# in_proj and x_proj behind the pair sums of a slot, in a fused Mamba and FFN kernel

## The chip, the cores and the metric

The kernel runs on one core of a Trainium2 chip. The metric is device time in microseconds from launch to end, the median of several runs. Matrix work runs on TensorE (PE; its weight loads are PEld), elementwise work and scans on VectorE (DVE), activations on ScalarE (ACT), the rest on GpSimd (POOL); SyncE (SP) issues the DMAs. All data is f32.

## What is computed

Four batches of 1024 tokens and 1024 channels. First a Mamba block: x is projected from the context (in_proj), goes through a short causal convolution and silu to u; x_proj makes from u the rows dt, B and C; then a scan along the tokens with 16 states for each channel, summed over the states with C. Its gate comes from the layer norm of x. Behind it stands an FFN with routing: logits over a whole batch choose two of eight experts, whose small hidden layers run on 16 heads, and a last 1024 x 1024 product with w3.

```python
x = einsum('ed,bld->bel', in_proj_w, ctx)            # in_proj
u = silu(causal_conv(x, conv_w) + conv_b)
x_dbl = einsum('ke,bel->bkl', x_proj_w, u)           # x_proj: dt_lo, Bm, Cm
delta = softplus(dt_proj_w @ dt_lo + dt_proj_b)
state = state * exp(delta * A) + (delta * u) * Bm    # for each token, 16 states
y = (state * Cm).sum(states) + D * u
x1 = x + y * silu(layernorm(x))
ffn: top 2 of softmax(layernorm(x1) @ switch_w); gelu MLP per head; (xn + o) @ w3 + b3
```

## The kernel before

The scan runs in 64 **steps**, 16 per batch: a step takes 512 tokens (half a batch, eight steps) and 128 channels. I number them 0 to 15 within a batch; steps 0 to 7 are the first half of the tokens, 8 to 15 the second. A step has eight **slots** q = 0 to 7, each for a pair of the 16 states. In a slot ScalarE makes two factors exp(delta A) (L1246); VectorE scans the two states (L1525) into one of three buffers `h`, and makes delta u times B for the next pair (L1501), except that in batch 0 TensorE makes it for five of the eight pairs (L948, from a transposed copy `duT`); GpSimd multiplies the pair with C (L865, "the product"); TensorE adds the pair to `yT` in PSUM (`sum_pair`, L962, "the sum"). A buffer `h` is free again three pairs later, when the sum is done.

Work for later steps is laid into slots by a table (`Schedule`): in_proj for the channels ten steps ahead (four matmuls of 512 columns, two passes each, L900) stands in slot 6 of most steps; in step 6 and step 14 slots 6 and 7 hold the two halves of x_proj for the next eight steps (L912), and in_proj follows in slot 0 of the next step. In_proj, x_proj, `v` (the matmul for delta, L921) and the transposes `zT` share PSUM bank S. In slot 1 (slot 2 of steps 7 and 15) of the next step ScalarE does the first tap of the convolution on in_proj's result (L1163 or L1172) and VectorE the other three (L1357). ScalarE's copies of the x_proj rows (L1184, L1185) stand at the head of slot 0, ahead of the exponentials. The FFN of one batch runs during the scans of the next: `hidden` (L1055), gelu on ScalarE (L1331, with a table load), `expert_out` (L1065), `out_add` (L1477), the logits (L1112) and the tiles with w3 (L1135).

Each engine is in order and goes through `slot(b, t)` for every batch b and slot t. For TensorE a slot had this order: in batch 0 the products with B; then a loop over the table's entries that holds in_proj, x_proj, zT, v, hidden and expert_out; in batch 0 in slot 7 the transposes of du_s (L929), which ScalarE copies to `duT` (L1209) in slot 0 of the next step, ahead of uD and of the next exponentials; then the sum of the pair one slot back (`sum_pair(g, q - 1)`, which waits for that pair's product); then a loop over the logits and tiles.

Of the kernel before, what the change touches and what calls it, by code (L numbers as in the profile page):

```python
# [16 lines left out]
J = DI // P  # L17
# [16 lines left out]
STEPS = TH * J  # L34
ALL = NB * STEPS
AHEAD = 10
# [223 lines left out]
PLAN = Schedule()  # L260


def build(nc, x, ctxT, w_inT, conv_w, conv_b, x_projT, dt_projT, dt_b, A_log, D, sw, sw_b,
# [4 lines left out]
    with ExitStack() as ctx:  # L268
# [210 lines left out]
        def count(b, *name):  # L479

            return PLAN.use[(b, *name)][1]
# [409 lines left out]
        def _(pe):  # L891
            e = pe

            def in_proj(loads, par, bank, wait):


                e.wait_ge(win_loaded[par], 1 + 16 * loads)
                e.wait_ge(evac[bank], 1 + wait)
                for k in range(DK):
                    mm = e.matmul(dense[:, bank, :], win[:, par, k, :], ctxs[:, k, :],  # L900
                                  start=(k == 0), stop=(k == DK - 1))
                mm.then_inc(xin_done, 1)
# [108 lines left out]
            def slot(b, t):  # L1011
# [9 lines left out]
                for what, *a in PLAN.slots[b][t]:  # L1021
# [35 lines left out]
                    elif what == "expert_out":  # L1057
# [7 lines left out]
                            mm = e.matmul(dense[HD * i:HD * i + HD, bank, :], w2s[:], hs_of(b, hp)[:, i, :],  # L1065
                                          start=True, stop=True)
                        mm.then_inc(o_done, 1)
                    elif what == "in_proj":
                        G = STEPS * b + a[0] + AHEAD
                        if G % J == 0:  # L1070
                            e.wait_ge(ctx_loaded, 1 + 16 * (G // J + 1))
                        in_proj((G - J) // 2 + 1, G % 2, S, count(b, *name))
                    elif what == "x_proj":
                        x_proj(c + 1, 1 - th, count(b, *name))
                    elif what == "x_proj_end":
                        x_proj_part(c + 1, range(J // 2, J))
                    elif what == "zT":
                        e.wait_ge(zn_done, 1 + g + 1)
                        e.wait_ge(evac[S], 1 + count(b, *name))
                        for k in range(TB):  # L1080
                            mm = e.transpose(dense[:, S, k * P:(k + 1) * P], xz[:, k * P:(k + 1) * P], ident[:])
                        mm.then_inc(zT_done, 1)
                    elif what == "v":
                        bo, th2, j2 = chunk_block(g + 1)
                        before_softplus(TH * bo + th2, j2, count(b, *name))
# [7 lines left out]
                    first_sum(g)  # L1093
                if b < NB and q >= 2:
                    sum_pair(g, q - 1)
                if b == 0 and q == SLOTS - 1:
                    times_b_at(N * g + 2 * q + 4)
                for what, *a in PLAN.slots[b][t]:
# [547 lines left out]
```

## Time and profile before

| | |
|---|---|
| three runs | 2474.52, 2473.86, 2465.63 us, median 2473.86 |
| the profiled execution | 2471.16 us, its span 2469.3 us |
| busy in the span | VectorE 2133.6 us (86%), TensorE 2013.5 (82%), ScalarE 1602.4 (65%), GpSimd 1445.2 (59%) |
| mean granted TensorE clock | 0.90 of full speed (2.4 GHz) |

The scans of the four batches fill the time from 95 to about 2283 us; after them a tail of 187 us finishes the FFN of the last batch, mostly on TensorE. A view of the profile that shows waits tells for how long an engine stood idle ahead of an instruction, and behind "<-" what released it. In the order of time a row may hold several instructions of one kind. A matmul's end in the trace is modelled and a little late, so work in sequence on TensorE is best timed from start to start.

### The profile page before, as it was taken

What the parts mean: (1) busy time and instruction counts of PE and PEld (TensorE: products, weight loads), DVE (VectorE), ACT (ScalarE), POOL (GpSimd) and SP (SyncE); (2) the same over time, 40 slices, a digit from 0 to 9 for tenths busy, and PEclk for the clock granted to TensorE, in tenths of its full rate; (3) what the DMA queues carried; (4) which work ended last, traced back from release to release, by engine and by line L of the source; (5) the groups of instructions that cost most, each with busy time, mean ns of one, the idle gap of its engine ahead of it and who ended that gap; (6) DMA issues with size and microseconds to landing.
All of it is one profiled execution on the core that took longest, in us unless ns stands there. A gap on an engine that the chain in (4) does not pass through costs nothing.

```text
span 2469.3 us, 32717 instructions
## 1 busy us (share of the span) xinstructions
PE 2013.5 (82%) x10776; PEld 1203.1 (49%) x10776; DVE 2133.6 (86%) x2712; ACT 1602.4 (65%) x2357; POOL 1445.2 (59%) x993
## 2 busy tenths in 40 slices
PE   6798888985757997996675897898685798797899
PEld 2677676653433553454453454454453455344344
DVE  5899789979999899998999899998999899999322
ACT  2677787656669868655667878855576857954500
POOL 0588677767756566566675566665775666665000
PEclk9899889997878998997888999899787899999899
DMA  5311434555612754566542464466460174578412
GB/s 174 128 37 52 150 99 148 188 162 169 246 37 103 261 166 133 161 204 203 188 155 74 140 232 152 147 224 199 154 239 26 60 253 145 164 251 283 168 56 72
DMA packets 200329, 383.01 MB, mean 155 GB/s; under 512 B 31553, under 2 KB 97089, under 8 KB 200162
## 3 DMA queue, kind: packets, MB, share of 16 engines
q1 hardware_dynamic: 196992, 380.47, 46.1%
q8 instruction: 86, 1.41, 0.2%
q10 hardware_dynamic: 3170, 0.47, 0.1%
q14 instruction: 81, 0.66, 0.1%
HBM read 346.80 MB, written 34.08 MB: 154 GB/s over the span
## 4 chain that ended last, share of the span: by engine, by line
PE 44%; DVE 19%; issue 17%; ACT 14%; POOL 3%; DMA 1%; DVEq 0%; SPq 0%; ACTq 0%; POOLq 0%
PE dense L1135 13%; PE dense L962 9%; DVE h L1525 9%; PE dense L900 5%; ACT dA L1246 4%; PE dense L948 3%; DVE dense L1501 3%; POOL h L865 3%; DVE u L1357 2%; PE dense L912 2%; PE dense L1112 2%; ACT L1213 2%; PE dense L921 2%; PE dense L1065 2%; PE dense L969 2%
## 5 line engine op out<-in xcount | busy, mean ns | idle before, releaser
L865 POOL TENSOR_TENSOR h<-h,Cb 128x1024 f32<-128x1024 f32 x512 | 1208.4, 2361 | 431.8 <-DVE h L1525 408.2
L1246 ACT ACTIVATE dA<-delta,Av 128x512 f32<-128x512 f32 x1024 | 703.1, 717 | 384.6 <-DVE h L1525 381.3
L962 PE MATMUL dense<-ident,h 128*128 128x128 f32 x4096 | 605.4, 299 | 165.0 <-POOL h L865 163.5
L962 PEld LDWEIGHTS dense<-ident,h 128*128 128x128 f32 x4096 | 521.1, 155 | 315.6 <-POOL h L865 225.8
L1525 DVE TENSOR_TENSOR_SCAN h<-dA,state,dense 128x512 f32<-128x512 f32 x512 | 627.4, 1263 | 31.0 <-issue 14.4
L1525 DVE TENSOR_TENSOR_SCAN h<-dA,dense 128x512 f32<-128x512 f32 x512 | 596.7, 1203 | 22.0 <-PE dense L962 8.5
L1501 DVE TENSOR_TENSOR dense<-dense,Bb 128x512 f32<-128x512 f32 x864 | 550.5, 682 | 1.6
L1135 PE MATMUL dense<-w3h,xT 128*128 128x512 f32 x832 | 386.0, 598 | 0.0
L859 POOL COPY state<-h 128x2 f32<-128x2 f32 x256 | 47.6, 186 | 336.6 <-DVE h L1525 335.1
L948 PE MATMUL dense<-Bb,duT 128*128 128x128 f32 x1280 | 179.9, 289 | 41.1 <-DVE h L1525 31.7
L1135 PEld LDWEIGHTS dense<-w3h,xT 128*128 128x128 f32 x832 | 147.9, 192 | 130.1 <-issue 130.1
L900 PE MATMUL dense<-ctxs,win 128*128 128x512 f32 x432 | 208.5, 628 | 2.2 <-ACT szT L1278 1.5
L948 PEld LDWEIGHTS dense<-Bb,duT 128*128 128x128 f32 x1280 | 160.4, 199 | 72.9 <-issue 65.6
L921 PE MATMUL dense<-dtaug,dtw 33*128 33x512 f32 x128 | 95.2, 832 | 110.2 <-DVE u L1357 108.5
L1357 DVE SCALAR_TENSOR_TENSOR u<-dense,cw,u 128x511 f32<-128x511 f32 (+2 forms) x192 | 140.7, 733 | 50.6 <-ACT u L1172 24.8
L1213 ACT ACT_TABLE_LOAD x113 | 145.0, 1283 | 2.0
L900 PEld LDWEIGHTS dense<-ctxs,win 128*128 128x128 f32 x432 | 84.2, 204 | 101.8 <-issue 101.8
L1112 PE MATMUL dense<-sww,row 128*32 128x256 f32 x1336 | 110.5, 417 | 1.2 <-ACT row L1287 1.2
L1065 PE MATMUL dense<-hs,w2s 128*64 128x512 f32 x224 | 72.8, 729 | 44.0 <-ACT hs L1331 41.4
L1202 ACT COPY dense<-du_s 128x512 f32<-128x512 f32 x64 | 37.5, 587 | 103.5 <-DVE dense L1501 103.3
L921 PEld LDWEIGHTS dense<-dtaug,dtw 33*128 33x128 f32 x128 | 24.5, 239 | 140.5 <-issue 140.4
L1487 DVE TENSOR_TENSOR res<-res,h 128x512 f32<-128x512 f32 x16 | 11.1, 691 | 88.1 <-PE dense L1135 88.1
(168 smaller groups left out, 2084.1 us busy)
## 6 DMA issues: line engine op xcount, KB each, us to landing
sww<-in_sw SPq DMA_DIRECT2D x167, 512.0 KB, 4.2
Cb<-bc_scratch SPq DMA_DIRECT2D x64, 512.0 KB, 6.1
Bb<-bc_scratch SPq DMA_DIRECT2D x54, 512.0 KB, 4.6
w3h<-in_sw SPq DMA_DIRECT2D x52, 512.0 KB, 8.2
w3h<-in_w3T SPq DMA_DIRECT2D x52, 512.0 KB, 5.2
row<-x_scratch SPq DMA_DIRECT2D x40, 512.0 KB, 4.5
xz<-in_x SPq DMA_DIRECT2D x64, 256.0 KB, 4.7
xt<-in_x SPq DMA_DIRECT2D x64, 256.0 KB, 3.9
```

Source lines behind the costliest of these rows:

```text
L865: e.tensor_tensor(h[:, s:s + 2, :], h[:, s:s + 2, :], Cb[:, 2 * q:2 * q + 2, :], ALU.mult).then_inc(prod_done, 1)
L900: mm = e.matmul(dense[:, bank, :], win[:, par, k, :], ctxs[:, k, :], start=(k == 0), stop=(k == DK - 1))
L921: e.matmul(dense[:, S, :], dtw[0:DR + 1, j * P:(j + 1) * P], dtaug[:], start=True, stop=True) \
L948: mm = e.matmul(dense[:, product_bank(g, n), k * P:(k + 1) * P], duT[:, g % 2, k, :], Bb[:, n, k * P:(k + 1) * P], start=True, stop=True)
L962: mm = e.matmul(yT[:, k, :], h[:, 2 * ((PAIRS * g + q) % RH) + i, k * P:(k + 1) * P], ident[:], is_transpose=True, start=False, stop=(q == ...
L1112: mm = e.matmul(dense[32 * n:32 * n + 32, F2, 0:32 * E], rows[:, lo:lo + 32], weights[:, :, 32 * n:32 * n + 32], start=first, stop=(k % TB ...
L1135: mm = e.matmul(dense[:, bank, :], xT_of(b, uu)[:, d, k * P:(k + 1) * P], w3[:, d, :], start=(b == NB and d == 0), stop=(d == J - 1), skip ...
L1213: e.preload_act_table_set("natural_log_exp_and_others")
L1246: e.activation(dA[:, i % RA, :], delta[:, st % 2, :], ACT.Exp, scale=Av[:, j * N + n:j * N + n + 1]).then_inc(dA_done, 1)
L1357: i = e.scalar_tensor_tensor(out=u[:, G % UR, s:T], in0=dense[:, bank, 0:T - s], scalar=cw[:, j, k:k + 1], in1=u[:, G % UR, s:T], op0=ALU. ...
L1501: e.tensor_tensor(dense[:, product_bank(g, n), :], du[:], Bb[:, n, :], ALU.mult).then_inc(duB_done, 1)
L1525: e.tensor_tensor_scan(h[:, 2 * ((PAIRS * g + q) % RH) + n % 2, :], dA[:, (N * g + n) % RA, :], dense[:, product_bank(g, n), :], state[:, ...
```

## The change

The three kinds of entries `in_proj`, `x_proj` and `x_proj_end` are taken out of TensorE's first loop and put into a loop of their own behind `sum_pair`, in the same slot. Waits, counts, banks and the table stay as they are, and so do the other engines' instructions. What stood behind these entries in the slot's first loop (`hidden`, `expert_out`, `turn`) and, in batch 0, the transposes of du_s in slot 7 now stand ahead of those of the same slot.

```diff
@@ -1065,15 +1065,6 @@
-                    elif what == "in_proj":
-                        G = STEPS * b + a[0] + AHEAD
-                        if G % J == 0:
-                            e.wait_ge(ctx_loaded, 1 + 16 * (G // J + 1))
-                        in_proj((G - J) // 2 + 1, G % 2, S, count(b, *name))
-                    elif what == "x_proj":
-                        x_proj(c + 1, 1 - th, count(b, *name))
-                    elif what == "x_proj_end":
-                        x_proj_part(c + 1, range(J // 2, J))
                     elif what == "zT":
@@ -1093,6 +1084,16 @@
                     first_sum(g)
                 if b < NB and q >= 2:
                     sum_pair(g, q - 1)
+                for what, *a in PLAN.slots[b][t]:
+                    if what == "in_proj":
+                        G = STEPS * b + a[0] + AHEAD
+                        if G % J == 0:
+                            e.wait_ge(ctx_loaded, 1 + 16 * (G // J + 1))
+                        in_proj((G - J) // 2 + 1, G % 2, S, count(b, what, *a))
+                    elif what == "x_proj":
+                        x_proj(c + 1, 1 - th, count(b, what, *a))
+                    elif what == "x_proj_end":
+                        x_proj_part(c + 1, range(J // 2, J))
                 if b == 0 and q == SLOTS - 1:
                     times_b_at(N * g + 2 * q + 4)
```

TensorE in an ordinary step of batch 0, from slot 5 on, before (L962 are the sums, eight matmuls for a pair; L948 the products with B; L900 in_proj; L929 the transposes of du_s):

```order
L962 MATMUL dense<-ident,h 128x128 x8
L948 MATMUL dense<-Bb,duT 128x128 x4
L962 MATMUL dense<-ident,h 128x128 x8
L900 MATMUL dense<-ctxs,win 128x512 x4
L962 MATMUL dense<-ident,h 128x128 x8
L929 MATMUL dense<-ident,du_s 128x128 x4
L962 MATMUL dense<-ident,h 128x128 x8
L948 MATMUL dense<-Bb,duT 128x128 x12
```

and the same place with the change:

```order
L948 MATMUL dense<-Bb,duT 128x128 x4
L962 MATMUL dense<-ident,h 128x128 x16
L900 MATMUL dense<-ctxs,win 128x512 x4
L929 MATMUL dense<-ident,du_s 128x128 x4
L962 MATMUL dense<-ident,h 128x128 x8
L948 MATMUL dense<-Bb,duT 128x128 x12
```

The sum of pair 5 has moved ahead of in_proj, next to that of pair 4 (x16); the transposes of du_s stand behind in_proj at once.

TensorE in step 6 of batch 0 and at the head of step 7, before (L912 are the halves of x_proj):

```order
L962 MATMUL dense<-ident,h 128x128 x8
L912 MATMUL dense<-u,xpw 64x512 x4
L962 MATMUL dense<-ident,h 128x128 x8
L912 MATMUL dense<-u,xpw 64x512 x4
L929 MATMUL dense<-ident,du_s 128x128 x4
L962 MATMUL dense<-ident,h 128x128 x8
L948 MATMUL dense<-Bb,duT 128x128 x8
L900 MATMUL dense<-ctxs,win 128x512 x4
L948 MATMUL dense<-Bb,duT 128x128 x4
L962 MATMUL dense<-ident,h 128x128 x8
```

and with the change:

```order
L962 MATMUL dense<-ident,h 128x128 x16
L912 MATMUL dense<-u,xpw 64x512 x4
L929 MATMUL dense<-ident,du_s 128x128 x4
L962 MATMUL dense<-ident,h 128x128 x8
L912 MATMUL dense<-u,xpw 64x512 x4
L948 MATMUL dense<-Bb,duT 128x128 x12
L962 MATMUL dense<-ident,h 128x128 x8
L900 MATMUL dense<-ctxs,win 128x512 x4
```

Ahead of the second half of x_proj now stand the sums of pairs 5 and 6 and the transposes; in_proj stands behind the sum of pair 7.

TensorE in step 6 of batch 1, where the slot also holds `expert_out` (L1065), before:

```order
L962 MATMUL dense<-ident,h 128x128 x8
L912 MATMUL dense<-u,xpw 64x512 x4
L1065 MATMUL dense<-hs,w2s 64x512 x2
L962 MATMUL dense<-ident,h 128x128 x8
L912 MATMUL dense<-u,xpw 64x512 x4
L962 MATMUL dense<-ident,h 128x128 x8
L900 MATMUL dense<-ctxs,win 128x512 x4
```

and with the change:

```order
L962 MATMUL dense<-ident,h 128x128 x8
L1065 MATMUL dense<-hs,w2s 64x512 x2
L962 MATMUL dense<-ident,h 128x128 x8
L912 MATMUL dense<-u,xpw 64x512 x4
L962 MATMUL dense<-ident,h 128x128 x8
L912 MATMUL dense<-u,xpw 64x512 x4
L962 MATMUL dense<-ident,h 128x128 x8
L900 MATMUL dense<-ctxs,win 128x512 x4
```

The first half of x_proj stands behind expert_out and the sum of pair 5, the second behind that of pair 6.

## Rows read from the trace of the kernel before

**Rows 1.** Busy time by stretches: stretch, us, PE, PEld, DVE, ACT, POOL, PEclk, DMA.
```profile
95.00:310.00 215.00, 189.42 (x1224) 153.08 (x1222) 185.97 (x205) 157.34 (x250) 165.67 (x134) 0.93 0.24 74
...
530.00:820.00 290.00, 200.40 (x1135) 123.57 (x1133) 272.03 (x355) 202.08 (x299) 185.71 (x148) 0.83 0.42 144
```

**Rows 2.** Who waited for whom, whole program: us in total, times, longest.
```profile
PEld dense L962 <- POOL h L865: 225.8, 126, 12.3
...
DVE h L1525 <- PE dense L962: 16.9, 26, 1.8
```

**Rows 3.** Order of time, batch 0, step 3: start us, us, engine, line.
```profile
178.59 3.60 PE L900 MATMUL dense<-ctxs,win 128*128 128x512 f32 x8
178.63 2.36 POOL L865 TENSOR_TENSOR h<-h,Cb 128x1024 f32<-128x1024 f32 x1
...
182.03 1.04 PE L962 MATMUL dense<-ident,h 128*128 128x128 f32 x8
...
182.90 0.60 PE L929 MATMUL dense<-ident,du_s 128*128 128x128 f32 x4
...
183.53 0.59 ACT L1209 COPY duT<-dense 128x512 f32<-128x512 f32 x1 [0.95 <-PE dense L929]
...
187.39 0.75 DVE L1357 SCALAR_TENSOR_TENSOR u<-dense,cw,u 128x511 f32<-128x511 f32 x1 [1.10 <-ACT u L1172]
```

**Rows 4.** Order of time, batch 0, steps 5 and 12, PE and POOL.
```profile
233.07 3.60 PE L900 MATMUL dense<-ctxs,win 128*128 128x512 f32 x8
...
233.11 2.36 POOL L865 TENSOR_TENSOR h<-h,Cb 128x1024 f32<-128x1024 f32 x1
...
450.68 4.69 POOL L865 TENSOR_TENSOR h<-h,Cb 128x1024 f32<-128x1024 f32 x2
...
452.88 3.70 PE L900 MATMUL dense<-ctxs,win 128*128 128x512 f32 x8
```

**Rows 5.** Order of time, batch 0, step 6 and the head of step 7.
```profile
260.38 2.36 POOL L865 TENSOR_TENSOR h<-h,Cb 128x1024 f32<-128x1024 f32 x1
260.43 3.65 PE L912 MATMUL dense<-u,xpw 128*64 128x512 f32 x8
...
268.71 0.57 ACT L1184 COPY dtaug<-dense 32x512 f32<-32x512 f32 x1 [5.65 <-PE dense L912]
...
279.27 0.69 DVE L1425 TENSOR_TENSOR szT<-dense,szT 128x512 f32<-128x512 f32 x1 [3.76 <-PE dense L962]
...
279.88 0.74 DVE L1357 SCALAR_TENSOR_TENSOR u<-dense,cw,u 128x511 f32<-128x511 f32 x1
```

**Rows 6.** Order of time, batch 1, step 6 and the head of step 7.
```profile
797.77 3.62 PE L912 MATMUL dense<-u,xpw 128*64 128x512 f32 x8 [0.57 <-ACT szT L1278]
...
801.59 1.08 PE L1065 MATMUL dense<-hs,w2s 128*64 128x512 f32 x4 [0.20 <-issue]
...
803.63 3.65 PE L912 MATMUL dense<-u,xpw 128*64 128x512 f32 x8
...
807.31 0.58 ACT L1184 COPY dtaug<-dense 32x512 f32<-32x512 f32 x1 [2.69 <-PE dense L912]
...
809.32 2.33 DVE L1525 TENSOR_TENSOR_SCAN h<-dA,dense 128x512 f32<-128x512 f32 x2 [2.18 <-issue]
```

**Rows 7.** Order of time, batch 1, step 14.
```profile
1088.13 2.35 POOL L865 TENSOR_TENSOR h<-h,Cb 128x1024 f32<-128x1024 f32 x1
...
1088.86 3.65 PE L912 MATMUL dense<-u,xpw 128*64 128x512 f32 x8
```

**Rows 8.** Order of time, batch 1, step 4 and the head of step 5.
```profile
725.79 2.35 POOL L865 TENSOR_TENSOR h<-h,Cb 128x1024 f32<-128x1024 f32 x1
...
726.05 4.66 PE L900 MATMUL dense<-ctxs,win 128*128 128x512 f32 x8
...
732.74 1.28 ACT L1331 ACT_TABLE_LOAD   x1 [0.60 <-PE dense L1055]
...
739.37 0.75 DVE L1357 SCALAR_TENSOR_TENSOR u<-dense,cw,u 128x511 f32<-128x511 f32 x1 [2.10 <-ACT u L1172]
```

## The prediction, made before the changed kernel ran

> **What bounds the kernel now.** I read the busy time by stretches first. While the scans run, VectorE is busy 186 of 215 us in the first half of batch 0 and 272 of 290 us in the first half of batch 1; TensorE is busy 189 of 215 and 200 of 290 us [rows 1]. VectorE sets the pace, and what matters is how late each thing is that its in-order queue waits for. The table of waits says where TensorE stands: before the pair sums (L962) its weight load waits 226 us in all for GpSimd's products, 126 times [rows 2]. So TensorE is often ahead of GpSimd at a sum, and that is the wait past which the change moves work. Then I read one ordinary step of batch 0 in order of time, around slot 6 [rows 3]: in_proj starts at 178.59, GpSimd's product of pair 5 starts at 178.63 and ends at 180.99, and the sum of pair 5 follows in_proj at 182.03 without a wait. The reader is to see that in_proj fills the 2.4 us in which TensorE would otherwise wait for the product.
>
> **An ordinary step of batch 0.** No instruction is added or removed. The sum of pair 5 now stands first: it starts when the product is there (180.99, and some 0.05 for the release), takes 0.87 (182.03 to 182.90, start to start), and in_proj's 3.44 (178.59 to 182.03) follow. The transposes of du_s (L929), queued behind both, begin at 185.35 and not at 182.90, 2.45 us later. Who waits for that: ScalarE's copy of duT (L1209) had already waited 0.95 for L929; behind it on its queue stand uD, two exponentials and the first conv tap, and VectorE's tap at 187.39 had waited 1.10 for the end of that row of work [rows 3]. No slack is left between in_proj and VectorE, so the step costs 2.45 in full. Nothing takes it back: TensorE's and GpSimd's work of slots 2 to 5 is released by VectorE's scans and moves with them. The sum that ends 1 us earlier helps nobody here, since VectorE doesn't wait for this sum: its old end is 183.07, and the two scans that need its buffer stand just ahead of the tap at 187.39, with no wait for TensorE.
>
> The price of a step is (end of the product of pair 5) - (old start of in_proj) + 0.05, where ScalarE waits for L929. Step 5 gives 233.11 + 2.36 - 233.07 + 0.05 = 2.45 [rows 4]. In step 12 logit matmuls keep TensorE later: two products stand in one row, the first ends at 450.68 + 2.35 = 453.03, in_proj started at 452.88, and the price is 0.2 [rows 4]. The same subtraction gives 2.8, 1.8, 2.7, 2.4, 2.4 and 2.4 for steps 0 to 5 (sum 14.6), 2.3, 1.5, 2.3 for steps 8 to 10 and 0.2, 0.2, 0.7 for 11 to 13 (sum 7.1); step 7 costs nothing, since ScalarE comes to the copy 1.9 us after its transposes. **21.7 us** in 12 steps.
>
> **The two x_proj steps of batch 0** (steps 6 and 14). x_proj's first half ran from 260.43 beside the product of pair 5 (260.38 + 2.36 = 262.74). Now the sum waits for the product, and the second half stands behind three things more: that wait of 2.36 (262.79 - 260.43), the transposes of du_s (0.5) and the sum of pair 6 (0.87): 3.7 us later. ScalarE's copy of the x_proj rows had already waited 5.65 for it [rows 5], and ahead of the next step's exponentials it stands in ScalarE's queue, so VectorE's scans come 3.7 later. There is a gain too: in_proj of slot 0 goes behind the sum of pair 7, for which VectorE had waited 3.76 before L1425. But VectorE's next instruction but that one is the tap (279.88), which needs that in_proj: the wait goes from the one to the other, and I get 283.8 for the tap, 3.9 later. Two such steps, 3.9 and 4.1: **8.0 us**.
>
> **The x_proj steps of batches 1 to 3.** In step 6 of a batch expert_out (L1065) stood behind x_proj in the slot and started at 801.59, when its gelu was there; x_proj had used the time from 797.77 on [rows 6]. Now expert_out and the sum stand first, x_proj starts at 801.59 + 1.01 + 0.9 = 803.5, and its second half at 803.5 + 3.6 + 0.9 = 808.0 and not at 803.63: 4.4 later. ScalarE had waited 2.69 for it and VectorE's scan at 809.32 had waited 2.18, so it is paid in full, three times: 13.2. In step 14 (batches 1 and 2) it is the wait for the product, 1088.13 + 2.35 + 0.05 - 1088.86 = 1.7, and the sum of pair 6, 0.87 [rows 7]: 2.5, twice, 5.1. Together **18.3 us**.
>
> **Ordinary steps of batches 1 to 3.** There is no du_s transpose there, and in_proj is wanted only by ScalarE's conv tap of the next step, which in every step stands further behind in_proj's old end than the delay would be. What is left is the FFN work behind it. In step 4 the first `hidden` stands in slot 7: the product ends at 725.79 + 2.35 = 728.14, in_proj started at 726.05, so hidden comes 2.1 later; ScalarE's gelu had waited 0.60 for it, and VectorE's tap behind it 2.10 for ScalarE [rows 8]. Three times: **6.4 us**. In seven more steps (5, 10 and 11) a gelu chain stands behind as well, with some slack ahead of it: between 0 and 2.1 each; I take 0.9, nearer to the middle, as ScalarE's queue is close there: **6.3 us**. In the second halves, where FFN tiles fill TensorE, the product is mostly ready when TensorE comes, and the order costs nothing.
>
> **Clock.** The new waits are idle time in TensorE, and TensorE's work may run at 1.2 GHz after them. At the lower level in_proj took 4.66 in step 4 of batch 1 [rows 8] and 3.60 in step 3 of batch 0 [rows 3]. With 8 large waits in batch 0 and 7 x_proj steps the bounds are 0 and 15 x 1.06 = 15.9 us. I take a third, **5.3 us**: of the steps of batch 0 none has a slow in_proj now, though TensorE waits in them.
>
> By the Trainium skill (TensorE: Matmul & The Clock Gate, section on HAM oscillation), waits between bursts of matmuls put the array back to the lower clock, and each next burst starts cold. That rule would take the upper bound of this term, 15.9, so 10.6 us more than the sum; it is the third rival.
>
> **Sum.** 21.7 + 8.0 + 18.3 + 6.4 + 6.3 + 5.3 = 66.0 us, on the profiled execution's 2471.2: 2537.2. The median of the three runs is 2.7 above that execution, so the forecast is 2540 us.
>
> **Rivals.**
> 1. Only the x_proj steps cost: the delay of the ordinary steps dies in a slack that I have missed, say because ScalarE catches up behind uD. 26.3 us, 2500 us with the 2.7. For it: in steps 7 and 15 it does die. Against it: the waits of 0.95 and 1.10 in a row [rows 3].
> 2. Faster: TensorE comes to slot 6 after the product, so that nothing is waited for, and the sums come 3.44 earlier while in_proj loses only 0.87 of its slack. Then VectorE's waits for sums go: 16.9 us [rows 2] and two waits like the 3.76 [rows 5], 24.4 us, 2449 us. It decides at the sign of (end of product - start of in_proj), which is negative in the second halves of batches 1 and 2 alone, where VectorE hardly waits for a sum.
> 3. The clock falls at each new wait and the sums and transposes behind it run slowly too: 10.6 to 26 us above the sum, 2551 to 2566 us.
> 4. The order doesn't matter, since TensorE takes what is ready: 2474 us. Against it: 226 us of waits of the sums' weight loads with other work queued behind [rows 2].
>
> By the Trainium skill (TensorE: Matmul & The Clock Gate, section on what each phase of a matmul is for) only weight loads are pulled ahead, and matmuls stay in program order, which speaks against rival 4; the trace agrees.
>
> **Chances.** Forecast 0.72 (2515 to 2562, from the bounds of the two estimated terms and some error in the others), rival 1 0.12, rival 3 beyond 2562 0.08, rival 2 0.04, rival 4 0.04. The range 2496 to 2563 holds the forecast and rival 1. A measurement tells about 0.5%, 12 us, from no change: faster 0.04, same 0.04, slower 0.92.
>
> **What the profile after should show.** In a step of batch 0: the sum of pair 5 (L962) waiting some 2.4 for L865, in_proj behind it, ScalarE's L1209 (one line further down) waiting 3.4 and not 0.95 for L929, VectorE's first tap waiting 3.5 and not 1.10, steps of 29.7 us and not 27.2. ScalarE's copy of x_proj rows waiting 9.4 in step 6 of batch 0 and 7 in that of batch 1. Steps 11 to 13 as before. The forecast is wrong if VectorE's waits before its tap don't grow, or if TensorE comes to slot 6 later than now, which would make the wait for the product vanish.

## The result, and the profile after

| | before | after |
|---|---|---|
| median of the runs | 2471.31 us (4 runs, 2465.63 to 2474.52) | 2577.18 us (4 runs, 2574.94 to 2581.58) |
| ratio, 95% interval | | 1.0435, 1.0421 to 1.0450 |
| span of the profiled execution | 2469.3 us | 2575.4 us |
| mean granted TensorE clock | 0.902 | 0.893 |

The change costs 106 us. The sign was forecast, the size was not: 2540 was the forecast, and 2577 lies above the upper end of 2563. In the kernel after, lines behind the moved entries are one further down, and zT is L1072.

First the table of waits after (who waited for whom: us in all, times, longest), against [rows 2]:

```profile
PEld dense L962 <- POOL h L865: 278.3, 149, 11.9
...
PEld dense L1065 <- ACT hs L1332: 79.2, 34, 4.6
...
DVE h L1526 <- issue: 64.8, 10, 10.6
...
DVE xT L1478 <- PE dense L1065: 59.5, 29, 7.0
...
DVE u L1358 <- ACT u L1173: 57.2, 18, 5.5
...
DVE u L1358 <- ACT u L1164: 41.9, 13, 12.9
```

The same of before, so far as it did not stand in [rows 2]:

```profile
PEld dense L1065 <- ACT hs L1331: 58.6, 31, 4.9
...
DVE xT L1477 <- PE dense L1065: 28.0, 21, 7.0
...
DVE u L1357 <- ACT u L1172: 24.8, 17, 3.9
DVE u L1357 <- ACT u L1163: 24.8, 10, 12.8
...
DVE h L1525 <- issue: 20.9, 8, 5.9
...
DVE h L1525 <- ACT dA L1246: 12.5, 11, 5.6
```

The sums wait 52 us more for GpSimd, as the change makes them. VectorE pays at three places. Its taps (u) wait 32 us more for ScalarE's L1173 and 17 us more for L1164, the first tap of the other steps. Its scans wait 44 us more in waits that the view calls "issue": seven of the ten, 8.4 to 10.7 us each, are the scans behind the x_proj rows, one for each x_proj step. Against that, the 12.5 us that scans had waited for exponentials (dA) fell to 0.9; two of those waits stood at the same place in batch 0. And `out_add` (xT) waits 31.5 us more for expert_out. The third was hardly in the forecast. The row of expert_out shows that it stands for longer at TensorE's head, waiting for its gelu (79 us, not 59).

An ordinary step of batch 0 in the kernel after, order of time (start us, us, engine, line), against [rows 3] and [rows 4]:

```profile
220.62 2.35 POOL L865 TENSOR_TENSOR h<-h,Cb 128x1024 f32<-128x1024 f32 x1
...
223.02 1.97 PE L962 MATMUL dense<-ident,h 128*128 128x128 f32 x8 [2.55 <-POOL h L865]
...
224.78 4.44 PE L900 MATMUL dense<-ctxs,win 128*128 128x512 f32 x8
...
229.06 0.60 PE L929 MATMUL dense<-ident,du_s 128*128 128x128 f32 x4
...
229.69 0.59 ACT L1210 COPY duT<-dense 128x512 f32<-128x512 f32 x1 [5.39 <-PE dense L929]
...
233.55 0.75 DVE L1358 SCALAR_TENSOR_TENSOR u<-dense,cw,u 128x511 f32<-128x511 f32 x1 [5.55 <-ACT u L1173]
```

The wait is the forecast one: the product ends at 222.97 and the sum starts at 223.02. What follows is slower than I had it. From start to start the sum takes 1.76 (before 0.87) and in_proj 4.28 (before 3.44). The transposes come 4.2 us later than before and not 2.45 later, and the tap waits 5.55 instead of 1.10.

The clock explains both figures. Busy time by stretches (stretch, us, PE, PEld, DVE, ACT, POOL, PEclk, DMA) of one step before, from in_proj on:

```profile
180.00:190.00 10.00, 8.89 (x63) 7.12 (x62) 8.90 (x12) 7.81 (x15) 8.54 (x7) 1.00 0.00 1
190.00:196.00 6.00, 4.22 (x19) 3.28 (x18) 6.00 (x8) 2.90 (x5) 3.89 (x4) 0.72 0.00 0
196.00:207.00 11.00, 11.00 (x89) 9.97 (x88) 9.82 (x10) 9.12 (x13) 10.04 (x9) 1.00 0.32 97
```

and after:

```profile
218.00:222.50 4.50, 2.47 (x23) 2.23 (x21) 4.22 (x6) 4.18 (x7) 4.36 (x4) 1.00 0.29 96
222.50:230.00 7.50, 6.98 (x25) 4.48 (x26) 5.50 (x6) 2.11 (x4) 7.26 (x7) 0.77 0.00 0
230.00:248.00 18.00, 14.71 (x116) 12.95 (x115) 14.42 (x16) 13.04 (x23) 10.27 (x10) 1.00 0.10 30
```

There is one stretch at 1.2 GHz in such a step either way. Before, it lies behind the taps, where TensorE has room. After, it lies on the sum and in_proj behind the new wait, where nothing has room, and the old place runs at full speed. That gives about 1 us back (VectorE's wait ahead of the delta product, 0.62, is gone, and that of a scan for a sum falls from 0.52 to 0.28). So a step grows by 3.44 and not by 2.45: 27.26 to 30.70 us for step 5, from its first scan to the next one.

Step 6 of batch 1 in the kernel after, against [rows 6]:

```profile
853.04 1.97 PE L1065 MATMUL dense<-hs,w2s 128*64 128x512 f32 x4 [4.39 <-ACT hs L1332]
...
861.97 3.65 PE L912 MATMUL dense<-u,xpw 128*64 128x512 f32 x8
...
865.65 0.58 ACT L1185 COPY dtaug<-dense 32x512 f32<-32x512 f32 x1 [9.59 <-PE dense L912]
...
867.66 2.33 DVE L1526 TENSOR_TENSOR_SCAN h<-dA,dense 128x512 f32<-128x512 f32 x2 [8.44 <-issue]
```

The scan waits 8.44 and not 2.18; I had forecast 4.4 more and it is 6.3 more.

The growth of the time from first scan to first scan, summed by batch, is the ruler for all runs below: 44.3 us in batch 0, then 23.5, 25.9 and 13.4, in all 107. The forecast had 29.7 for batch 0 and 31.0 for the others, and 5.3 for the clock.

### The profile page after: what moved, and what is told of

Read it like the earlier page. It is cut to its first block, busy times and chain, and to the rows that moved or that the text cites. A ratio compares the mean times of both kernels' runs of the same rounds, so it can differ in the third digit from the quotient of the medians.

```text
span 2575.4 us, 32717 instructions
## 1 busy us (share of the span) xinstructions
PE 2040.2 (79%) x10776; PEld 1211.9 (47%) x10776; DVE 2133.5 (83%) x2712; ACT 1602.1 (62%) x2357; POOL 1445.5 (56%) x993
## 3 DMA queue, kind: packets, MB, share of 16 engines
q1 hardware_dynamic: 196992, 380.47, 44.3%
## 4 chain that ended last, share of the span: by engine, by line
PE 34%; DVE 20%; issue 19%; ACT 13%; POOL 11%; DMA 1%; DVEq 0%; SPq 0%; POOLq 0%; ACTq 0%
DVE h L1526 10%; PE dense L1136 10%; POOL h L865 9%; PE dense L962 6%; PE dense L900 6%; ACT dA L1247 4%; DVE dense L1502 3%; PE dense L912 2%; DVE u L1358 2%; PE dense L1065 2%; ACT L1332 2%; ACT L1214 2%; PE dense L1055 2%; PE dense L969 2%; ACT hs L1332 1%
## 5 line engine op out<-in xcount | busy, mean ns | idle before, releaser
L865 POOL TENSOR_TENSOR h<-h,Cb 128x1024 f32<-128x1024 f32 x512 | 1208.5, 2361 | 468.0 <-DVE h L1526 444.4
L962 PE MATMUL dense<-ident,h 128*128 128x128 f32 x4096 | 612.8, 302 | 203.7 <-POOL h L865 202.4
L962 PEld LDWEIGHTS dense<-ident,h 128*128 128x128 f32 x4096 | 523.5, 156 | 355.8 <-POOL h L865 278.3
L900 PE MATMUL dense<-ctxs,win 128*128 128x512 f32 x432 | 219.2, 655 | 0.7 <-ACT dtw L1186 0.7
L948 PE MATMUL dense<-Bb,duT 128*128 128x128 f32 x1280 | 181.0, 291 | 47.8 <-DVE h L1526 36.8
L948 PEld LDWEIGHTS dense<-Bb,duT 128*128 128x128 f32 x1280 | 161.5, 201 | 79.7 <-issue 69.7
L900 PEld LDWEIGHTS dense<-ctxs,win 128*128 128x128 f32 x432 | 89.6, 219 | 93.9 <-issue 93.9
L1065 PE MATMUL dense<-hs,w2s 128*64 128x512 f32 x224 | 80.1, 798 | 66.6 <-ACT hs L1332 65.5
L1113 PE MATMUL dense<-sww,row 128*32 128x256 f32 x1336 | 104.5, 394 | 5.8 <-DMA sww<-in_sw 5.4
L1332 ACT ACT_TABLE_LOAD x49 | 62.9, 1283 | 63.0 <-PE dense L1055 62.7
```

Source lines behind the costliest of these rows:

```text
L865: e.tensor_tensor(h[:, s:s + 2, :], h[:, s:s + 2, :], Cb[:, 2 * q:2 * q + 2, :], ALU.mult).then_inc(prod_done, 1)
L948: mm = e.matmul(dense[:, product_bank(g, n), k * P:(k + 1) * P], duT[:, g % 2, k, :], Bb[:, n, k * P:(k + 1) * P], start=True, stop=True)
L962: mm = e.matmul(yT[:, k, :], h[:, 2 * ((PAIRS * g + q) % RH) + i, k * P:(k + 1) * P], ident[:], is_transpose=True, start=False, stop=(q == ...
L1332: e.activation(hs_of(b, hp)[:, i, :], dense[:, bank, :], ACT.Gelu, bias=b1s[:]) \
```

## The experiments

Every ratio is against runs of the kernel before on the same chip (medians 2469.5 to 2471.0). The kernel after was not run again with them: a difference from it is taken from its 2577.18 us.

### One part of the change at a time

**in_proj alone behind the sum.** x_proj stays in the first loop of the kernel before.

```diff
-                    elif what == "in_proj":
...
                     sum_pair(g, q - 1)
+                for what, *a in PLAN.slots[b][t]:
+                    if what == "in_proj":
...
```

> Only in_proj goes behind the sum; both halves of x_proj stay ahead of it. If each wait costs only its own length (the prediction's prices), this is 21.7 + 6.4 + 6.3 = 34 us over the kernel before. If TensorE's clock falls in the wait and the sum and in_proj behind it run at 1.2 GHz, a step of batch 0 costs 3.4 as in the trace of after and not 2.45, and the kernel comes to 55 to 65 us over the kernel before.

Measured: 2533.55 us, ratio 1.0254 (1.0229 to 1.0279), +62.5. By batch: 28.1, 8.5, 16.4, 5.9.

**x_proj alone behind the sum.**

```diff
-                    elif what == "x_proj":
-                        x_proj(c + 1, 1 - th, count(b, *name))
-                    elif what == "x_proj_end":
...
                     sum_pair(g, q - 1)
+                for what, *a in PLAN.slots[b][t]:
+                    if what == "x_proj":
...
```

> Only the two halves of x_proj go behind the sums; in_proj stays ahead. By the prediction's prices 3.7 twice and 18.3, so 26 us over the kernel before. If the clock adds to it, 40 to 50 us: in step 6 of batches 1 to 3 VectorE's scan then waits some 6 longer than before, and not 4.4. If this and the kernel with in_proj alone add up to after's 106, the two parts don't interact.

Measured: 2525.88 us, ratio 1.0221 (1.0198 to 1.0243), +54.9. By batch: 15.3, 13.3, 15.6, 10.6. This is above the 40 to 50 that I had for the clock. Both parts cost about twice what waits alone would by my prices, and together a little more than the whole change (117 and 106). I read that as the clock at first. The later runs show that in batches 1 to 3 most of it is another wait, that of expert_out.

**The second half of x_proj alone.**

```diff
-                    elif what == "x_proj_end":
-                        x_proj_part(c + 1, range(J // 2, J))
...
                     sum_pair(g, q - 1)
+                for what, *a in PLAN.slots[b][t]:
+                    if what == "x_proj_end":
+                        x_proj_part(c + 1, range(J // 2, J))
```

> The kernel before with only the second half of x_proj put behind the sum of pair 6 (in batch 0 also behind the transposes of du_s). That product is ready when TensorE comes, so there is no new wait and the clock has no reason to fall: the price is the length of what it is moved past, 0.87 in five steps and 0.87 + 0.5 in two: 7 us over the kernel before. If moving x_proj costs more than the lengths and waits say, as the 55 us for both halves would let one think (7.8 a step), it is 15 us or more.

Measured: 2481.86 us, ratio 1.0052 (1.0036 to 1.0067), +12, between the 7 and the 15 or more. So some 43 of the 55 us come with the first half, which stands behind expert_out and the sum of pair 5.

### Is it the clock?

**More work in the wait.** The kernel after, and in slot 6, ahead of the slot's first loop, two of the four matmuls of the coming in_proj or x_proj, whose result the full product overwrites later.

```diff
+                for what, *a in PLAN.slots[b][t] if q == 6 else ():
+                    if what == "in_proj":
...
+                        for k in range(2):
+                            e.matmul(dense[:, S, :], win[:, G % 2, k, :], ctxs[:, k, :], start=(k == 0), stop=(k == 1))
```

> After, with extra work: in slot 6, at the head of TensorE's slot, the first two of the four matmuls of in_proj (or of x_proj's first half) are done once more into the same bank, and overwritten by the real ones behind the sum. They take 1.7 us at full speed and lie inside waits of 2.4 (batch 0) and 4.4 us. If the clock makes the difference, this kernel with more work is 20 to 35 us faster than after (2542 to 2557), sums behind the wait take 0.87 and not 1.76, and a step of batch 0 costs 2.45. If the clock isn't it, the time is after's, 2577, or more.

Measured: 2562.50 us, ratio 1.0373 (1.0348 to 1.0397): 15 us faster than the kernel after, with 1.7 us more work at each of 55 places. In steps 3 to 5 of batch 0 the sum now waits 0.6 to 0.9 and takes 0.93, so the low clock is gone there. But in step 6 the growth stays at 8.9, and step 2 grows by 6.7: the clock falls at other places. The gain is less than I expected.

**The same work in the kernel before**, as its control (the same added lines):

> The kernel before with the same two extra matmuls at the same place. They put off all that stands behind them by 1.7 us and leave no wait. If a delay of in_proj and of the du_s transposes is paid in full in batch 0, 12 ordinary steps and 7 x_proj steps cost 1.7 each, 33 us, and the gelu steps up to 10 more: 2505 to 2515. If those delays had slack, under 2485.

Measured: 2538.08 us, ratio 1.0264 (1.0237 to 1.0290), +67, where I had expected 34 to 44. So 1.7 us more ahead of the sum costs 1.2 us a place in the mean, but it is not spread evenly: 28.7, 18.3, 18.3 and 2.2 us by batch. Steps 0 and 1 of batches 1 to 3 don't grow at all, while steps 5 and 7 of batches 1 and 2 grow by 3.0 to 3.6. TensorE has next to no slack at the end of a step in batch 0 and in some steps with FFN work, and has it elsewhere. The same matmuls that cost 67 us here bring 15 in the kernel after, where many of them stand in a wait.

**A filler ahead of x_proj only**, in step 6 of batches 1 to 3, in the wait of expert_out (four more matmuls, overwritten as well).

```diff
+                for what, *a in PLAN.slots[b][t] if b and st == J - 2 else ():
+                    if what == "x_proj":
...
+                        for k in range(4):
+                            e.matmul(dense[0:DR + 2 * N, S, :], xpw[:, k, :], u[:, (J * (c + 1) + k) % UR, :],
+                                     start=(k == 0), stop=(k == 3))
```

> After, and in slot 6 of step 6 of batches 1 to 3 alone the four matmuls of x_proj's first half are done once more at the head of the slot, into the bank that the real ones overwrite. They fill the wait of 4.4 us ahead of expert_out. By the clock theory expert_out, the sum and the first half of x_proj then run at full speed: from the start of expert_out to the end of x_proj's second half it takes 10.2 us and not 12.5, 2.3 less three times, so 7 us less than after (2570). If the extra delay there has another cause, such as the order of the queue itself, the 12.5 stay.

Measured: 2569.20 us, ratio 1.0404 (1.0388 to 1.0420), −8, as expected. Step 6 of batch 1, against the rows of after above:

```profile
851.70 1.08 PE L1072 MATMUL dense<-hs,w2s 128*64 128x512 f32 x4 [0.20 <-issue]
852.71 1.10 PE L962 MATMUL dense<-ident,h 128*128 128x128 f32 x8
...
853.74 3.65 PE L912 MATMUL dense<-u,xpw 128*64 128x512 f32 x8
...
862.02 0.58 ACT L1192 COPY dtaug<-dense 32x512 f32<-32x512 f32 x1 [7.29 <-PE dense L912]
```

With TensorE busy until the gelu is there, expert_out takes 1.01 from start to start and not 1.90, the sum 1.03 and not 1.90, and ScalarE waits 7.29 and not 9.59. The 2.3 us between these are the low clock in such a step; 7.29 is what the order alone makes, close to my 7.

**GpSimd's product earlier.** GpSimd makes du_s behind the product of pair 5 instead of pair 4, so that this product is ready sooner.

```diff
-                    if q == 4 and g + 1 < ALL:
+                    if q == 5 and g + 1 < ALL:
                         du_of(g + 1, 1 + count(b, "v", st) + 1)
```

> After, with GpSimd's product for du_s (1.27 us) taken one slot later, so behind the product of pair 5 and not ahead of it: that product ends 1.3 us earlier, and TensorE's wait for it in slot 6 of batch 0 shrinks from 2.55 to 1.3. Prices by waits alone: 1.3 us less in each of 9 ordinary steps and 4 x_proj steps, 17 us less than after (2560). If the clock is what doubles the price, the shorter wait also spares the slow sum (0.9 and not 1.76) and the slow in_proj, another 1 to 1.7 in the steps of batch 0: 2545 to 2552.

Measured: 2567.52 us, ratio 1.0375 (1.0348 to 1.0402), −10 (three runs at 2567 to 2571, one at 2553), a miss for both theories. The same step of batch 0:

```profile
220.91 1.09 PE L962 MATMUL dense<-ident,h 128*128 128x128 f32 x8 [0.35 <-POOL h L865]
...
221.84 3.60 PE L900 MATMUL dense<-ctxs,win 128*128 128x512 f32 x8
...
229.76 0.75 DVE L1358 SCALAR_TENSOR_TENSOR u<-dense,cw,u 128x511 f32<-128x511 f32 x1 [1.67 <-ACT u L1173]
```

and its busy time by stretches:

```profile
218.00:230.50 12.50, 12.02 (x84) 9.54 (x82) 10.07 (x13) 9.44 (x17) 11.11 (x9) 1.00 0.07 22
230.50:243.00 12.50, 9.43 (x38) 7.44 (x39) 10.48 (x13) 7.13 (x11) 8.72 (x8) 0.64 0.11 26
```

The wait at the sum is all but gone (0.35), sum and in_proj run at full clock, and the tap waits 1.67. Yet steps 3 to 5 are as long as in the kernel after (30.7 us). The low stretch has gone back to its old place behind the taps and is far longer there (0.64 over 12.5 us, where it was 0.72 over 6). VectorE pays there now: its wait ahead of the delta product went from 0.62 to 1.28, and those of its scans in the step from 0.52 to 2.51. In both kernels the low stretch begins every 30.72 us, step after step: after at 192.33, 223.05 and 253.77, here at 203.22, 233.94 and 264.66. So the length of a step isn't only the sum of the waits that one can point at. Why the clock stays down for longer here, and whether the length of a step and the clock hold each other, these runs don't show. The 11 us that batch 0 gains all the same lie in steps 6 to 14.

**The same edit in the kernel before**, as its control:

> The kernel before with the one edit of the run that made GpSimd's du_s behind the product of pair 5 instead of pair 4, as its control. In the kernel before the transposes that read du_s start some 3 us after it would be ready now, and the sum of pair 5 stands behind in_proj, which ends after its product either way. If the edit costs nothing by itself: 2471, within 5 us, and then the 10 us that it took off the kernel after are all it is worth there. If making du_s later costs something by itself (ScalarE's copy of du_s comes a slot later, TensorE waits for it in x_proj steps): 2476 to 2490, and the gain in the kernel after is larger by that.

Measured: 2469.71 us, ratio 0.9999 (0.9989 to 1.0009). Making du_s later costs nothing by itself.

### What stands behind the wait in batch 0?

**Transposes of du_s earlier, kernel before.** In batch 0, but for the x_proj steps, they go from slot 7 to the head of slot 6, ahead of in_proj.

```diff
+                if b == 0 and q == SLOTS - 2 and g + 1 < STEPS and j != J - 2:
+                    turn_du(g + 1)
                 for what, *a in PLAN.slots[b][t]:
...
-                if b == 0 and q == SLOTS - 1 and g + 1 < STEPS:
+                if b == 0 and q == SLOTS - 1 and g + 1 < STEPS and j == J - 2:
                     turn_du(g + 1)
```

> The other way round, from the kernel before: the transposes of du_s in batch 0 stand at the head of slot 6, ahead of in_proj and the sum, and not in slot 7 (step 6 and 14 as before). ScalarE's copy of duT no longer waits 0.95 to 2.7 for them, so VectorE's waits before the first tap (1.1 in steps 1 to 6, 0.3 to 1.8 in steps 11 to 14) shrink to 0.2. By the theory that this chain is on the path in batch 0 it is 8 to 11 us faster than the kernel before, 0.4%; if that chain has slack, no difference.

Measured: 2454.22 us, ratio 0.9938 (0.9924 to 0.9951), −15 (−17 by the profiled spans), more than the 8 to 11 that I had expected: faster than both kernels. Steps 3 to 5 lose 2.0 us each, the whole of the tap's 1.10 and more. The more is the clock: the low stretch behind the taps no longer comes in these steps, and with it go the 0.62 ahead of the delta product and half of the scan's 0.52. Busy time by stretches there:

```profile
190.00:203.00 13.00, 12.89 (x88) 10.39 (x88) 12.69 (x14) 10.89 (x17) 12.62 (x11) 1.00 0.26 82
```

This is the step that the prediction rests on, read from the other side: what VectorE's tap waits for is in_proj, transposes and copy in a row.

**The same edit in the kernel after:**

> The kernel after with the transposes of du_s at the head of slot 6 in batch 0 (not in x_proj steps), ahead of the waiting sum. Their 0.6 to 0.9 us on TensorE and the 0.6 us copy on ScalarE leave the chain from the product of pair 5 to the tap, in about 13 steps. If that chain is what an ordinary step of batch 0 pays for: 1.3 us a step, 17 us in all, 2560. If instead the low clock settles with the length of a step, so that a wait taken away at one place comes back at another: within 6 us of the kernel after, 2571 to 2577. If the transposes cut the clock's fall as well: 2.5 to 3.5 us a step, 2535 to 2548.

Measured: 2540.49 us, ratio 1.0288 (1.0271 to 1.0305), −37, which lies in the last of the three ranges: the transposes cut the clock's fall as well. Batch 0 now costs 6.4 us over the kernel before instead of 44.3; batches 1 to 3 are unchanged (23.5, 25.9, 13.3). One step:

```profile
208.66 1.89 PE L962 MATMUL dense<-ident,h 128*128 128x128 f32 x8 [2.03 <-POOL h L865]
...
209.84 0.56 ACT L1212 COPY duT<-dense 128x512 f32<-128x512 f32 x1
...
210.34 4.52 PE L900 MATMUL dense<-ctxs,win 128*128 128x512 f32 x8
...
216.49 0.75 DVE L1360 SCALAR_TENSOR_TENSOR u<-dense,cw,u 128x511 f32<-128x511 f32 x1 [2.85 <-ACT u L1175]
```

Even in this step, where the clock falls, the tap waits 2.85 and not 5.55: copy, uD and two exponentials are done before in_proj ends. In most other steps of batch 0 the sum takes 0.93. Of the 37 us, some 17 are what the same edit brings in the kernel before. The other 20 are what the transposes bring behind the new wait only: they no longer stand behind the delayed in_proj, they shorten the sum's wait from 2.55 to 2.03, and in steps 0, 2 and 5 sum and in_proj run at full clock (0.93 and 3.44). The runs don't part the order from the clock here.

### What stands behind which wait in batches 1 to 3?

Batches 1 to 3 cost 62.7 us where I had 31.0. Step 5 of batch 1 before:

```profile
760.67 3.67 PE L900 MATMUL dense<-ctxs,win 128*128 128x512 f32 x8 [0.57 <-ACT szT L1278]
...
764.49 1.08 PE L1065 MATMUL dense<-hs,w2s 128*64 128x512 f32 x4
...
766.52 1.13 PE L1055 MATMUL dense<-xT,w1s 64*128 64x512 f32 x4
...
773.66 0.75 DVE L1477 SCALAR_TENSOR_TENSOR xT<-dense,b2s,xT 128x512 f32<-128x512 f32 x1 [0.21 <-PE dense L1065]
```

and after:

```profile
812.01 1.98 PE L1065 MATMUL dense<-hs,w2s 128*64 128x512 f32 x4 [4.39 <-ACT hs L1332]
...
815.68 4.24 PE L900 MATMUL dense<-ctxs,win 128*128 128x512 f32 x8
...
819.85 1.13 PE L1055 MATMUL dense<-xT,w1s 64*128 64x512 f32 x4
...
824.83 0.75 DVE L1478 SCALAR_TENSOR_TENSOR xT<-dense,b2s,xT 128x512 f32<-128x512 f32 x1 [3.21 <-PE dense L1065]
```

Before, in_proj filled the wait of expert_out for its gelu to 0.1 us. After, expert_out waits 4.39 with in_proj queued behind it, and from expert_out to the next `hidden` it is 7.84 us and not 2.03. Of these 5.8 us, 3.6 are in_proj at its usual pace and 2.2 the low clock: expert_out 1.91 and not 1.01, the sum 1.76 and not 1.02, in_proj 4.17 and not some 3.6.

**in_proj ahead of expert_out again.** The kernel after, but in slot 6 of steps 5, 10 and 11 of batches 1 to 3 in_proj has its old place (seven in_projs, not eight: in batch 3 only step 5 has one).

```diff
+                    elif what == "in_proj" and b and t in (46, 86, 94):
...
+                        in_proj((G - J) // 2 + 1, G % 2, S, count(b, *name))
...
-                    if what == "in_proj":
+                    if what == "in_proj" and not (b and t in (46, 86, 94)):
```

> The kernel after, but in the three places of batches 1 to 3 where in_proj's slot also holds expert_out (slot 6 of steps 5, 10 and 11, eight in_projs) in_proj stands in its old place, ahead of expert_out. In step 5 the profile after has expert_out waiting 4.39 us for its gelu, a wait that in_proj used to fill; hidden behind in_proj comes 5.2 us later than before, where I had put 0 to 2.1 as bounds. If that wait is what the ordinary steps of batches 1 to 3 pay for: about 4.4 in each of three step 5s and 3 in each of four steps 10 and 11, 20 us less with some given back, 2552 to 2562. If it is only the granted clock: 0 to 6 us less, 2570 to 2577. If these steps pay for the sum of pair 5 alone: the same as the latter.

Measured: 2555.27 us, ratio 1.0345 (1.0327 to 1.0362), −22, as expected for the wait of expert_out and not for the clock alone. Batches 1 to 3 now cost 13.4, 15.6 and 9.6, that is 24.1 less. The last out_add of step 5 waits for nothing that the view shows (it waited 3.21 in the kernel after).

**The first half of x_proj ahead of expert_out again**, in step 6 of batches 1 to 3.

```diff
+                    elif what == "x_proj" and b and t == 54:
+                        x_proj(c + 1, 1 - th, count(b, *name))
...
-                    elif what == "x_proj":
+                    elif what == "x_proj" and not (b and t == 54):
```

> The kernel after, but in step 6 of batches 1 to 3 the first half of x_proj stands in its old place, ahead of expert_out; the second half and all else stay as after. The three steps cost 10.2, 10.3 and 10.8 us in the kernel after, and some 3 us more each in step 8 may hang on them. The second half alone behind its sum cost 0.5 to 1.5 in these steps. If the wait of expert_out for its gelu is what pays: 8 to 9 us less in each, 24 to 34 us less, 2543 to 2553. If the cost hangs on the second half behind two more sums: 3 to 8 less, 2569 to 2574.

Measured: 2555.40 us, ratio 1.0348 (1.0331 to 1.0365), −22. Batches 1 to 3 cost 15.6, 16.7 and 8.3, in all 22.1 less: a little less than I had expected, but far more than the rival gave. ScalarE waits 3.69 for the x_proj rows in batch 1, the scan behind it 3.18:

```profile
858.65 0.57 ACT L1187 COPY dtaug<-dense 32x512 f32<-32x512 f32 x1 [3.69 <-PE dense L912]
...
860.65 2.33 DVE L1528 TENSOR_TENSOR_SCAN h<-dA,dense 128x512 f32<-128x512 f32 x2 [3.18 <-issue]
```

**All three edits** (transposes at the head of slot 6, in_proj and x_proj ahead of expert_out), in the kernel after:

> The kernel after with the three edits of e10, e13 and e14 together: transposes of du_s at the head of slot 6 in batch 0, and in_proj or x_proj in its old place where its slot holds expert_out. Each sum of pair 5 elsewhere still stands ahead of in_proj. The three took 37, 22 and 22 us off. If they are three separate places: 2577 less 81, 2496, within 6. If they share a cause, such as a low clock that any one of them lifts: 2505 to 2530. What is left over the kernel before is then what waiting for the sum itself costs.

Measured: 2502.93 us, ratio 1.0135 (1.0113 to 1.0156). The three took 37, 22 and 22 us off, 81; together they take 74, between my two expectations. They are nearly separate places; some 7 us overlap. Batch 0 costs 7.4 over the kernel before, the others 9.1, 12.0 and 2.6.

### What beats both kernels

**The second half of x_proj earlier, kernel before:** in slot 6, behind the first half and ahead of the sum. In batch 0 and in step 14 the halves stand together; in step 6 of batches 1 to 3 expert_out stands between them.

```diff
-                self.add(b, t + 7, "x_proj_end", st // J)
+                self.add(b, t + 6, "x_proj_end", st // J)
...
+                for what, *a in PLAN.slots[b][t]:
+                    if what == "x_proj_end":
+                        x_proj_part(c + 1, range(J // 2, J))
```

> The kernel before with the second half of x_proj in slot 6, directly behind the first half and ahead of the sum of pair 5. The copies of the x_proj rows on ScalarE can start 3 to 5 us earlier in the seven x_proj steps, whose waits hold the next exponentials: 12 to 20 us less, 2451 to 2459. Against it stands the sum of pair 5, which comes 3.6 us later and frees the buffer for the first scan of the next step: if that decides, 2471 within 5 us or slower, up to 2485.

Measured: 2461.99 us, ratio 0.9963 (0.9949 to 0.9978), −8, between the two. ScalarE's waits for the x_proj rows fall from 33.6 us to 19.3 (seven times); 3.6 us are given back at waits of the scans for the late sum and 4.8 at those for exponentials:

```profile
DVE h L1526 <- PE dense L962: 20.5, 26, 1.6
ACT dtaug L1185 <- PE dense L912: 19.3, 7, 4.7
DVE h L1526 <- ACT dA L1247: 17.3, 16, 3.9
```

**Both** (transposes and second half earlier):

> The kernel before with both: transposes of du_s at the head of slot 6 in batch 0, and the second half of x_proj directly behind the first. If the two gains are at different places they add: 2454 less what the second half alone brings, 2434 to 2442. If the second half brings nothing by itself: 2450 to 2458.

Measured: 2441.53 us, ratio 0.9880 (0.9864 to 0.9897). Together they gain 29 us (15 and 8 alone): the fastest kernel here. Both edits go against the change: they bring forward what others wait for, and leave the sum until its product is there.

## Why the forecast was wrong in size

- **What bounds the kernel, and where TensorE waits:** right. The sum of pair 5 waits 2.55 for L865 (2.4 forecast), and in_proj had filled that wait. The end of a step has no slack in batch 0, as the control with more work showed (28.7 us for 16 places); in the first steps of the later batches it has.
- **An ordinary step of batch 0, 2.45 each:** the wait was right, the price too low. The chain in_proj, transposes, duT, tap grew by 4.45, of which 1 came back elsewhere, so 3.44. L1210 waits 5.39 and not 3.4, the tap 5.55 and not 3.5, a step takes 30.7 and not 29.7. Where logits keep TensorE later, the price held: about 0.2 and 0.4 for steps 11 and 12 (0.2 and 0.2 forecast). Batch 0 in all: 44.3, with x_proj steps, where 29.7 were forecast.
- **The x_proj steps of batch 0, 8.0 us:** some 14 were measured: in steps 6 and 7 growth is 11.7, of which 3.5 belong to in_proj's tap, and in steps 14 and 15 it is 6.5, of which 0.6. The copy waits 11.38 in step 6 and not 9.4, since the sum and the first half ran at the low clock (1.88 and 4.35 from start to start). And VectorE's wait did not just pass from L1425 to the tap: it waits 1.73 at the first, 3.60 at the second, and 1.46 for products with B (L948) that ran at 1.2 GHz behind the late copy.

```profile
295.81 0.57 ACT L1185 COPY dtaug<-dense 32x512 f32<-32x512 f32 x1 [11.38 <-PE dense L912]
...
310.06 0.75 DVE L1358 SCALAR_TENSOR_TENSOR u<-dense,cw,u 128x511 f32<-128x511 f32 x1 [3.60 <-ACT u L1164]
```

- **"Clock", 5.3 us:** the first step that failed. My reason was that no in_proj of batch 0 was slow although TensorE waits in these steps. But there was already a stretch at 1.2 GHz in each of steps 3 to 6, behind the taps, where it cost about 1 us. The new wait moves it onto the sum and in_proj. And I had counted only in_proj or x_proj as slow (1.06), not the sum (0.89) nor expert_out (0.90) between the wait and them. Nor is 1.06 the most that an in_proj loses: that of step 8 takes 5.13 from start to start, 1.69 more than 3.44, and the 4.66 was an in_proj only in part at the lower clock. In batch 0 14.6 us were missing. Of these, 5.2 lie in what the ordinary steps 0 to 5 cost more than their price, where the low clock costs 1.7 a step and gives 0.9 back, and 6.1 in the x_proj steps, where it is part of it; that the clock is most of the 14.6 is read from these rows and not shown by a run. In step 6 of a later batch it is 2.3 us, and there the run with filler shows it. The rule of the Trainium skill that I had set against the row (TensorE: Matmul & The Clock Gate, section on HAM oscillation) says that each burst behind a wait starts cold; for the sums behind these waits the trace agrees in steps 0 to 7 of batch 0 (1.2 to 1.9 us and not 0.9) and disagrees in steps 8 to 10, where the sum waits 1.9 to 2.1 and takes 0.93. In step 8 the clock falls only afterwards, in in_proj.
- **"In seven more steps (5, 10 and 11) … between 0 and 2.1 each":** the second failed step, and the larger. 6.3 us were forecast and in_proj ahead of expert_out takes 24.1 back. The bound looked only at the wait for the product. In these slots in_proj was moved past expert_out as well, whose wait for the gelu it had filled; the bound should have been its whole 3.6 us, plus the clock. I had made this very step for x_proj ("expert_out and the sum stand first") and not for in_proj.
- **x_proj steps of batches 1 to 3:** the mechanism was right; the 4.4 in step 6 was 6.3 at the scan, of which 2.3 are clock (ScalarE's copy waits 9.59 and not 7), and 0.9 at an out_add besides. 13.2 were forecast for the three, and the first half in its old place takes back 22.1. Some of that is a growth of 2.9 us in step 8 of batches 1 and 2 (VectorE waits for a tile there), which I had not priced and whose chain I haven't followed. Step 14 came out as forecast: 5.5 us for two, 5.1 forecast.
- **Step 4, 6.4 us:** right in size (7.5 us in the run where only it and the x_proj step are left ahead of step 6), wrong in place. VectorE pays at out_add (2.90), and its tap waits 2.10 as before.
- **Rivals:** rival 3 (the clock falls at each new wait, 2551 to 2566) was nearest in mechanism and still too low, as it knew nothing of expert_out's wait. Rivals 1, 2 and 4 are refuted by the time.

The account of the 106 us: the transposes behind the new wait in batch 0 make 20 of them (with what they do to the clock), in_proj behind the wait of expert_out 22, x_proj behind it 22, some 7 of these 64 counted twice. The remaining 49 are the difference between the run with all three edits (2503) and the kernel before with its one (2454): waiting at the sum itself, the clock behind it, and the second half of x_proj behind the sum of pair 6, which alone cost 12 in the kernel before. How the 49 split into these was not separated by a run of its own.

## What to carry to other kernels

Work that is moved in an in-order queue is moved past every instruction in between: for each one ask what it waits for, and whether the moved work had filled that wait. Here the wait for the product was seen and that of expert_out for its gelu, in the same slot, was not, and it cost about as much. As an upper bound, price the work behind a new wait on TensorE at 1.2 GHz, all of it up to the instruction that others wait for, and look where the low stretch of the clock lies now, since it may move. The first thing to bring forward is what heads another engine's chain (the transposes, x_proj's second half); the last is what only frees a buffer.

## What the runs showed of the hardware

- A wait of 2.55 us once in a step of 30.7 us was enough to have the following sum at 1.76 us and in_proj at 4.28, whereas waits of 1.91 and 2.13 us in steps 9 and 10 left both at full clock (0.93 and 3.44 to 3.53). The length of the wait alone doesn't decide: in the kernel after, behind a wait of 2.01 us in step 0 of batch 1 the sum takes 1.76, and behind one of 2.04 in step 1 it takes 0.93:

```profile
632.13 1.97 PE L962 MATMUL dense<-ident,h 128*128 128x128 f32 x8 [2.01 <-POOL h L865]
...
665.56 1.09 PE L962 MATMUL dense<-ident,h 128*128 128x128 f32 x8 [2.04 <-POOL h L865]
```

- More matmuls can make a kernel faster: 1.7 us of work without use at each of 55 places took 15 us off the kernel after, and cost 67 in the kernel before, which mostly had no wait there.
- The clock can take a gain away. With the product earlier, the wait at the sum fell from 2.55 to 0.35 us and the step stayed at 30.7 us, since the stretch at the lower clock grew from 0.72 over 6 us to 0.64 over 12.5 us at another place.
